# Half-row product pairs for the small corner of an fp32r split, in a mixture-of-experts stage on TensorE

## The chip, the cores and the metric

One of the cores of one Trainium2 chip runs the whole program. The metric is the device time of one execution in microseconds (us); lower is better. The profile is one more execution, with every instruction recorded.

## What is computed

The reference is an image-and-text model with two layers. Image patches are embedded and joined with looked-up text rows to 8 x 141 = 1128 tokens of width 192. Then come a two-way state-space block with a feed-forward, a quantized feed-forward, an attention of 12 heads, and a mixture of experts. The change is in the last, which computes with `flat` = 1128 x 192, hidden width 768:

```python
def _expert(xf, W1, W2, W3):
    gate = jnp.minimum(xf @ W1, LIMIT)
    up = jnp.clip(xf @ W3, -LIMIT, LIMIT)
    return jax.nn.silu(gate) * up @ W2
scores = jnp.sqrt(jax.nn.softplus(flat @ gate_w))
_, indices = jax.lax.top_k(scores + gate_bias, K)        # K = 2 of 8 experts
...
y = _expert(flat, w1s, w2s, w3s)                          # shared expert
# routed: the same with w1, w2, w3 of each token's two experts, weighted and added
```

## The kernel before

Five engines run hand-written queues, tied by semaphores. The experts' part, at the end, is a list `ITEMS` of 21 items: five "shared" ones (the shared expert on 256 tokens, the last on 128), then sixteen "routed" ones, each 256 slots of tokens that one expert has been given. `SLOTS` is 256, `KH` is 6, `P` is 128, `DA` and `DB` are 128 and 64 (the width 192 is cut at 128).

**A step.** An item has six steps (`n = g * KH + m`), each for 128 of the 768 hidden columns: a gate half (q = 0) and an up half (q = 1), each summed in its own PSUM bank (`bank[2 * (n % 2) + q]`), so that two steps can be in flight. The function `up` (L1880 on) issues the steps on TensorE.

**The split.** The products are in fp32r, a reduced form that runs in one pass. To keep accuracy, tokens and weights are split in a lead (the value rounded to fp32r) and a rest (value minus lead). Rows 0 to 127 of the width take three products: lead x lead (L1909), lead x rest of the tokens (L1910), rest of the weights x lead (L1911). The last 64 rows of the width fill only half of the 128 rows, so they are laid down twice: `x_both` holds the tokens' lead in partitions 0 to 63 and their rest in 64 to 127, and the weights' block (`2 * P` to `4 * P` of its columns) holds the same 64 rows twice. L1912 multiplies the weights' lead with `x_both`, which gives lead x lead and lead x rest at once; L1913 multiplies the weights' rest with `x_both`, which gives rest x lead and, in the other half, rest x rest, a term that L1909 to L1911 leave out. That makes five products of 128 rows, 128 output columns and 256 moving columns per half, ten per step.

**Who makes the operands.** ACT's `lead_x(g)` (L1276) copies the tokens of item g to `x_lead` (L1287) and to the lower half of `x_both` (L1288), each with a count on the semaphore `x_lead`; DVE's `rest_x` (L2715) waits for the two counts and subtracts to `x_rest` (L2725) and to the upper half of `x_both` (L2726), with counts on `x_rest`, for which `up` waits. Both are double buffered. For routed items the source is PSUM: POOL gathers token rows by indirect DMA (L844), and TensorE turns them (`turn_slots`, L1932 and L1933). ACT's `lead_w` (L1298) rounds a step's weights four steps ahead, DVE's `rest_w` (L2732) makes the rest two steps ahead; `w_lead` and `w_rest` have four buffers. The experts' weights come by indirect DMA from POOL (L823), three buffers deep, asked for when an earlier item has been finished.

**What follows a step.** ACT takes Silu of the gate half (L1328) after the fifth product, DVE clips the up half (L2655) after the tenth and multiplies both (L2666). TensorE's step n waits for Silu and clip of step n - 2 (`g_silu`, `u_clip`).

**Order on TensorE.** `up(g)`, then the turning of the next routed item's tokens, then `down(g - 1)` (L1949, two times six f32 products of 192 columns, recorded as 24; half as many for the item with 128 tokens), then `up(g + 1)`. In the shared items the router's small work is put between steps: the gate products (L1872 with 128 rows and L1873 with 64), the counting (L1903, L1904) and the placing products (L1919) in the fifth item; the router's arithmetic stands between the steps of DVE's queue. ACT's order after an item's last Silu and `lead_w` is `lead_x(g + 1)`, then `output(g - 1)` (L1315), which waits for the down projection.

**Other places that the prediction reads.** The attention's score products (L1754) have 64 rows: for each pair of heads one product reads partitions 0 to 63 and the next 64 to 127, into two banks; an f32 product is recorded as two. Before and behind them stand fp32r projections of 128 rows (L1716 to L1720, 282 columns). L1774 and L1775 are transposes of 128 and 96 rows. L1633 and L1634 are a feed-forward's f32 products, of 128 rows and, for the bias, of one row.

Of the kernel before, what the change touches and what calls it, by code (L numbers as in the profile page):

```python
# [17 lines left out]
P = 128  # L18
# [56 lines left out]
def build(nc, i, out):  # L75
    ctx = ExitStack()
    with ctx:
# [52 lines left out]
        def reduced(name, at, width, end, size):  # L130

            return nc.alloc_sbuf_tensor_at(name, [P, width], F32R, offset=end - 4 * (size - at))
# [51 lines left out]
        def lead_rest(name, base, at, width, dt):  # L184
# [158 lines left out]
        XH = [reduced(f"x_lead{k}", KH * SLOTS * 2 + k * SLOTS, SLOTS, big2_end, N2) for k in range(2)]  # L343
        XR = [reduced(f"x_rest{k}", KH * SLOTS * 2 + (2 + k) * SLOTS, SLOTS, big2_end, N2) for k in range(2)]
        XB = [reduced(f"x_both{k}", KH * SLOTS * 2 + (4 + k) * SLOTS, SLOTS, big2_end, N2) for k in range(2)]
        WAT = [(KH * SLOTS * 2 + 6 * SLOTS + k * 2 * BLK, big2_end, N2) for k in range(2)] \
            + [(1024 + k * 2 * BLK, creg_end, 5120) for k in range(2)]
        WH = [reduced(f"w_lead{k}", at, BLK, end, size) for k, (at, end, size) in enumerate(WAT)]
# [530 lines left out]
        def _(act):  # L879
# [395 lines left out]
            def lead_x(g):  # L1275

                kind, c = ITEMS[g]
                w = TOK(kind, c)
                if kind == "shared":
                    a, b = XTa[:, c * SLOTS:c * SLOTS + w], XTb[0:DB, c * SLOTS:c * SLOTS + w]  # L1280
                else:
                    act.wait_ge(S["slots_turned"], c + 1)
                    o = bank[6 + c % 2]
                    a, b = o[:, 0:SLOTS], o[0:DB, SLOTS:2 * SLOTS]
                if g >= 2:
                    act.wait_ge(S["gu_mm"], 2 * KH * (g - 1))
                nc.scalar.copy(XH[g % 2][:, 0:w], a).then_inc(S["x_lead"], 1)  # L1287
                nc.scalar.copy(XB[g % 2][0:DB, 0:w], b).then_inc(S["x_lead"], 1)  # L1288

            def lead_w(n):  # L1290

# [56 lines left out]
        def _(pe):  # L1348
# [531 lines left out]
            def up(g):  # L1880
# [1 line left out]
                kind, c = ITEMS[g]  # L1882
                w = TOK(kind, c)
                pe.wait_ge(S["x_rest"], 2 * (g + 1))
                xh, xr, xb = XH[g % 2][:, 0:w], XR[g % 2][:, 0:w], XB[g % 2][:, 0:w]
                for m in range(KH):
                    n = g * KH + m
                    if kind == "routed":
# [12 lines left out]
                    if n == KH + 5:  # L1901
                        pe.wait_ge(S["picked"], 1)
                        mm(bank[7][:, 0:RT], before[:, :], MB[:, :, :].rearrange("p t e -> p (t e)"), start=True, stop=True)  # L1903
                        mm(bank[7][:, RT:2 * RT], ones[:, :], MB[:, :, :].rearrange("p t e -> p (t e)"), start=True, stop=True)\  # L1904
                            .then_inc(S["counted"], 1)
                    for q in range(2):
                        o = bank[2 * (n % 2) + q][:, 0:w]
                        a, b = slice(q * P, (q + 1) * P), slice((2 + q) * P, (3 + q) * P)
                        mm(o, wh[:, a], xh, start=True, stop=False)  # L1909
                        mm(o, wh[:, a], xr, start=False, stop=False)  # L1910
                        mm(o, wl[:, a], xh, start=False, stop=False)  # L1911
                        mm(o, wh[:, b], xb, start=False, stop=False)  # L1912
                        mm(o, wl[:, b], xb, start=False, stop=True).then_inc(S["gu_mm"], 1)  # L1913
                    if n == PLACED:
                        pe.wait_ge(S["spread"], 3)
                        o = bank[6][:, 0:2 * CHUNKS]
# [7 lines left out]
            def turn_slots(j):  # L1924

                pe.wait_ge(ld_slots[j % 2], 16 * GCH * (j // 2 + 1))
                if j >= 2:
                    pe.wait_ge(S["x_rest"], 2 * (FIRST + j - 1))
                o = bank[6 + j % 2]
                for q in range(GCH):  # L1930
                    x = XG[:, j % 2, q * D:(q + 1) * D]
# [33 lines left out]
        def _(dve):  # L1965
# [749 lines left out]
            def rest_x(g):  # L2715
# [5 lines left out]
                else:  # L2721
                    o = bank[6 + c % 2]
                    a, b = o[:, 0:SLOTS], o[0:DB, SLOTS:2 * SLOTS]
                dve.wait_ge(S["x_lead"], 2 * (g + 1))
                v.tensor_tensor(XR[g % 2][:, 0:w], a, XH[g % 2][:, 0:w], ALU.subtract).then_inc(S["x_rest"], 1)  # L2725
                v.tensor_tensor(XB[g % 2][DB:P, 0:w], b, XB[g % 2][0:DB, 0:w], ALU.subtract).then_inc(S["x_rest"], 1)  # L2726

# [233 lines left out]
```

## Time and profile before

| | us |
|---|---|
| median of 3 runs | 735.29 |
| lowest, highest | 730.75, 736.48 |
| the profiled execution | 732.9 |
| its span, first to last instruction | 730.9 |
| mean granted clock of TensorE over the span | 0.934 of full |

Engines: PE is TensorE's products, PEld its weight loads, which overlap them, DVE is VectorE, ACT ScalarE, POOL GpSimd. Times in rows are us from the span's start, unless marked ns. A timeline row gives start, length, engine, line, operation, out<-in, shapes, count of merged instructions and, in brackets, the engine's idle time before it and what released it. Products are pipelined and their ends are modelled: their lengths overlap, and starts say more than lengths. A granted clock of 1.00 is TensorE's higher level, 2.4 GHz.

### The profile page before, as it was taken

Reading aid. Unit: us, or ns where it says so; the run is one execution under the profiler, and the core shown is the slowest. Engines: PE = TensorE matmul, PEld = TensorE weight load, DVE = VectorE, ACT = ScalarE, POOL = GpSimd, SP = SyncE. Lnnn points to the kernel's source line nnn. Section 1 sums busy time; section 2 is a strip of 40 time slices with the busy share of each in tenths; the row PEclk is TensorE's granted clock in tenths of the full one; section 3 lists DMA queues with packets and bytes.
Section 4 is the critical chain, followed back from the end, with each engine's and each line's share of the span. In section 5 each row is a group of like instructions: output and inputs, shape, how many; then the busy total and the mean of one; then the engine's idle time right before and its main releaser. Section 6 shows DMA issues by size and latency. Waiting matters only on the chain.

```text
span 730.9 us, 13424 instructions
## 1 busy us (share of the span) xinstructions
PE 633.8 (87%) x4912; PEld 566.1 (77%) x4912; DVE 490.0 (67%) x1269; ACT 383.2 (52%) x875; POOL 277.1 (38%) x292
## 2 busy tenths in 40 slices
PE   3759898899899556568999999989999999999993
PEld 3659775569898432357888888979999999999993
DVE  3668688674604877657777785488587768677761
ACT  1349876873433466455665643442255656556540
POOL 5340525344301415042323353001244756666633
PEclk9959999999999756679999999999999999999997
DMA  6600000215000580300000110103095876768733
GB/s 181 120 1 5 1 1 1 98 50 147 1 0 1 148 150 0 120 0 5 4 4 4 25 72 2 48 1 120 19 320 153 250 234 198 261 177 254 200 95 69
DMA packets 27585, 64.67 MB, mean 88 GB/s; under 512 B 5951, under 2 KB 19152, under 8 KB 25184
## 3 DMA queue, kind: packets, MB, share of 16 engines
q0 software_dynamic: 12640, 46.90, 21.8%
q1 hardware_dynamic: 13116, 16.04, 8.3%
q10 hardware_dynamic: 1764, 0.88, 0.5%
q8 instruction: 39, 0.64, 0.4%
q14 instruction: 26, 0.21, 0.1%
HBM read 58.55 MB, written 5.74 MB: 88 GB/s over the span
## 4 chain that ended last, share of the span: by engine, by line
PE 46%; DVE 6%; issue 2%; ACT 2%; POOL 1%; DMA 0%; POOLq 0%; DVEq 0%; ACTq 0%
PE bank L1949 11%; PE bank L1909 4%; PE bank L1912 4%; PE bank L1913 4%; PE bank L1910 4%; PE bank L1911 4%; PE bank L1818 2%; PE bank L1754 2%; PE bank L1797 2%; DVE amx L2559 1%; PE bank L1774 1%; PE bank L1804 1%; PE bank L1716 1%; PE bank L1780 1%; DVE big L2565 1%
## 5 line engine op out<-in xcount | busy, mean ns | idle before, releaser
L2655 DVE TENSOR_SCALAR big<-bank 128x256 f32<-128x256 f32 (+1 forms) x126 | 52.3, 415 | 52.9 <-PE bank L1913 52.6
L1328 ACT ACTIVATE big<-bank 128x256 f32<-128x256 f32 (+1 forms) x126 | 47.5, 379 | 48.9 <-PE bank L1913 48.9
L811 POOL TENSOR_TENSOR big<-big,arc 128x423 f32<-128x423 f32 (+1 forms) x48 | 37.8, 814 | 73.6 <-DVE arc L2579 73.6
L837 POOL DMA_INDIRECT total<-big,goal x32 | 54.1, 1692 | 23.9 <-issue 17.5
L1909 PE MATMUL bank<-x_lead,w_lead 128*128 128x256 f32 x192 | 56.4, 294 | 0.0
L1912 PE MATMUL bank<-x_both,w_lead 128*128 128x256 f32 x192 | 54.4, 283 | 0.0
L1913 PE MATMUL bank<-x_both,w_rest 128*128 128x256 f32 x192 | 54.1, 282 | 0.0
L1911 PE MATMUL bank<-x_lead,w_rest 128*128 128x256 f32 x192 | 54.1, 282 | 0.0
L1910 PE MATMUL bank<-x_rest,w_lead 128*128 128x256 f32 x192 | 54.0, 281 | 0.0
L2666 DVE SCALAR_TENSOR_TENSOR big<-big 128x256 f32<-128x256 f32 (+1 forms) x126 | 50.4, 412 | 0.0
L844 POOL DMA_INDIRECT big<-x_rows,origin x32 | 34.0, 1061 | 33.9 <-DVE goal L2712 20.1
L1298 ACT CAST w_lead<-wreg 128x512 fp32r<-128x512 f32 x60 | 37.2, 620 | 14.0 <-DMA wreg<-in_e_gate_up,expert 6.7
L2732 DVE TENSOR_TENSOR w_rest<-wreg,w_lead 128x512 fp32r<-128x512 f32 x60 | 41.6, 693 | 0.3
L2559 DVE TENSOR_REDUCE amx<-bank 128x3 f32<-128x423 f32 (+1 forms) x48 | 25.9, 540 | 22.9 <-PE bank L1754 15.2
L1949 PE MATMUL bank<-wreg,big 128*128 128x192 f32 x240 | 40.7, 326 | 0.0
L1949 PEld LDWEIGHTS bank<-wreg,big 128*128 128x128 f32 x240 | 38.8, 190 | 0.0
L1315 ACT ACTIVATE big<-bank,share 128x192 f32<-128x192 f32 x32 | 11.8, 418 | 50.9 <-PE bank L1949 50.9
L1909 PEld LDWEIGHTS bank<-x_lead,w_lead 128*128 128x128 f32 x192 | 36.5, 190 | 0.3 <-DVE x_both L2726 0.2
L1912 PEld LDWEIGHTS bank<-x_both,w_lead 128*128 128x128 f32 x192 | 36.5, 190 | 0.0
L1913 PEld LDWEIGHTS bank<-x_both,w_rest 128*128 128x128 f32 x192 | 36.4, 190 | 0.0
L1910 PEld LDWEIGHTS bank<-x_rest,w_lead 128*128 128x128 f32 x192 | 36.4, 189 | 0.0
L1911 PEld LDWEIGHTS bank<-x_lead,w_rest 128*128 128x128 f32 x192 | 36.3, 189 | 0.0
(542 smaller groups left out, 2022.9 us busy)
## 6 DMA issues: line engine op xcount, KB each, us to landing
big<-in_patches SPq DMA_DIRECT2D x2, 768.0 KB, 8.6
areg<-in_e_gate_up SPq DMA_DIRECT2D x1, 1536.0 KB, 6.5
shared_lead<-in_e_gate_up POOLq DMA_DIRECT2D x1, 1536.0 KB, 7.2
wreg<-in_ffn_w SPq DMA_DIRECT2D x1, 1152.0 KB
ffw_lead<-in_ffn_w POOLq DMA_DIRECT2D x1, 1152.0 KB, 7.8
out<-total SPq DMA_DIRECT2D x2, 423.0 KB
wreg<-in_in_w SPq DMA_DIRECT2D x2, 419.0 KB
wreg<-in_in_w SPq DMA_DIRECT2D x4, 209.5 KB
```

The lines of the kernel that those rows point to most:

```text
L811: pool.tensor_tensor(o, o, arc[0:r, 18 * (b % 2) + 3 * g:18 * (b % 2) + 3 * g + q].unsqueeze(2).to_broadcast([r, q, L]), ALU.mult).then_in ...
L837: pool.indirect_dma_start(out=total, in_=YS[:, j % 2, q * D:(q + 1) * D], in_offset=None, out_offset=bass.IndirectOffsetOnAxis(ap=goal[:, ...
L1328: nc.scalar.activation(GS[:, n % 3, 0:w], bank[2 * (n % 2)][:, 0:w], ACT.Silu).then_inc(S["g_silu"], 1)
L1909: mm(o, wh[:, a], xh, start=True, stop=False)
L1910: mm(o, wh[:, a], xr, start=False, stop=False)
L1911: mm(o, wl[:, a], xh, start=False, stop=False)
L1912: mm(o, wh[:, b], xb, start=False, stop=False)
L1913: mm(o, wl[:, b], xb, start=False, stop=True).then_inc(S["gu_mm"], 1)
L1949: last = mm(result(g, q), HH[:, g % 2, at:at + P], W[:, W2 + k * D:W2 + (k + 1) * D], start=k == 0, stop=k == KH - 1)
L2655: v.tensor_scalar(UM[:, n % 3, 0:w], bank[2 * (n % 2) + 1][:, 0:w], 10.0, -10.0, ALU.min, ALU.max).then_inc(S["u_clip"], 1)
L2666: v.scalar_tensor_tensor(out=HH[:, g % 2, m * SLOTS:m * SLOTS + w], in0=GS[:, n % 3, 0:w], scalar=SILU_LIMIT, in1=UM[:, n % 3, 0:w], op0=A ...
L2732: v.tensor_tensor(WL[n % 4][:, :], weights(g)[:, m * BLK:(m + 1) * BLK], WH[n % 4][:, :], ALU.subtract)\
```

## The change

Per step, the two products with `x_both` and the weights' rest (L1913, once for each half) go. In their place, ahead of the step's other products, stand two products of 64 rows: the gate's with the lower half of the weights' rest and of `x_both`, the up half's with the upper half of the weights' rest and a second copy of the tokens' lead in partitions 64 to 127 (`x_upper`, two buffers, in free room of `creg`). They open the two sums (`start=True`); the other eight products follow as before, and the gate half's last one is now the sixth of the step, the up half's the tenth. The term rest x rest of the last 64 rows is no longer in the sum. ACT's `lead_x` makes three copies in place of two, the waits on `x_lead` count by three, and TensorE's `up` and `turn_slots` wait for it as well.

```diff
+        XU = [reduced(f"x_upper{k}", 3200 + k * SLOTS, SLOTS, creg_end, 5120) for k in range(2)]
...
                 nc.scalar.copy(XH[g % 2][:, 0:w], a).then_inc(S["x_lead"], 1)
                 nc.scalar.copy(XB[g % 2][0:DB, 0:w], b).then_inc(S["x_lead"], 1)
+                nc.scalar.copy(XU[g % 2][DB:P, 0:w], b).then_inc(S["x_lead"], 1)
...
                 pe.wait_ge(S["x_rest"], 2 * (g + 1))
-                xh, xr, xb = XH[g % 2][:, 0:w], XR[g % 2][:, 0:w], XB[g % 2][:, 0:w]
+                pe.wait_ge(S["x_lead"], 3 * (g + 1))
+                xh, xr, xb, xu = XH[g % 2][:, 0:w], XR[g % 2][:, 0:w], XB[g % 2][:, 0:w], XU[g % 2][:, 0:w]
...
+                    gu = [bank[2 * (n % 2) + q][:, 0:w] for q in range(2)]
+                    mm(gu[0], wl[0:DB, 2 * P:3 * P], xb[0:DB], start=True, stop=False)
+                    mm(gu[1], wl[DB:P, 3 * P:4 * P], xu[DB:P], start=True, stop=False)
                     for q in range(2):
-                        o = bank[2 * (n % 2) + q][:, 0:w]
                         a, b = slice(q * P, (q + 1) * P), slice((2 + q) * P, (3 + q) * P)
-                        mm(o, wh[:, a], xh, start=True, stop=False)
-                        mm(o, wh[:, a], xr, start=False, stop=False)
-                        mm(o, wl[:, a], xh, start=False, stop=False)
-                        mm(o, wh[:, b], xb, start=False, stop=False)
-                        mm(o, wl[:, b], xb, start=False, stop=True).then_inc(S["gu_mm"], 1)
+                        mm(gu[q], wh[:, a], xh, start=False, stop=False)
+                        mm(gu[q], wh[:, a], xr, start=False, stop=False)
+                        mm(gu[q], wl[:, a], xh, start=False, stop=False)
+                        mm(gu[q], wh[:, b], xb, start=False, stop=True).then_inc(S["gu_mm"], 1)
...
                 if j >= 2:
                     pe.wait_ge(S["x_rest"], 2 * (FIRST + j - 1))
+                    pe.wait_ge(S["x_lead"], 3 * (FIRST + j - 1))
...
-                dve.wait_ge(S["x_lead"], 2 * (g + 1))
+                dve.wait_ge(S["x_lead"], 3 * (g + 1))
```

## Rows read from the trace of the kernel before

**Rows 1.** Page, part 1: busy us (share of the span), instructions by engine.

```profile
PE 633.8 (87%) x4912; PEld 566.1 (77%) x4912; DVE 490.0 (67%) x1269; ACT 383.2 (52%) x875; POOL 277.1 (38%) x292
```

**Rows 2.** Stretches: length, busy us and instructions by engine, granted clock, DMA share, GB/s.

```profile
542.73:703.72 160.99, 160.99 (x1233) 160.83 (x1233) 122.61 (x282) 94.70 (x222) 95.21 (x77) 1.00 0.72 213
355.00:440.00 85.00, 83.28 (x944) 72.35 (x943) 66.01 (x172) 47.33 (x137) 32.58 (x40) 1.00 0.07 23
```

**Rows 3.** Chain of waits from 566 to 600: its shares by line.

```profile
by line: PE bank L1949 33.5%; PE bank L1912 12.8%; PE bank L1909 12.6%; PE bank L1913 12.6%; PE bank L1910 12.6%; PE bank L1911 12.5%; PE bank L1932 1.9%; PE bank L1933 1.9%
```

**Rows 4.** Timeline of PE, one routed item: start, length, engine, line, out<-in.

```profile
577.16 0.41 PE L1909 MATMUL bank<-x_lead,w_lead 128*128 128x256 f32 x1
...
578.47 0.28 PE L1909 MATMUL bank<-x_lead,w_lead 128*128 128x256 f32 x1
...
579.66 0.28 PE L1909 MATMUL bank<-x_lead,w_lead 128*128 128x256 f32 x1
...
584.86 4.07 PE L1949 MATMUL bank<-big 128*128 128x192 f32 x24
588.62 0.41 PE L1909 MATMUL bank<-x_lead,w_lead 128*128 128x256 f32 x1
```

**Rows 5.** Timeline of DVE in that item; [idle before <-releaser].

```profile
579.86 0.42 DVE L2655 TENSOR_SCALAR big<-bank 128x256 f32<-128x256 f32 x1 [0.16 <-PE bank L1913]
...
581.13 0.42 DVE L2655 TENSOR_SCALAR big<-bank 128x256 f32<-128x256 f32 x1
...
586.45 0.42 DVE L2726 TENSOR_TENSOR x_both<-bank,x_both 64x256 fp32r<-64x256 f32 x1
```

**Rows 6.** Timeline of ACT in that item.

```profile
577.57 0.73 ACT L1315 ACTIVATE big<-bank,share 128x192 f32<-128x192 f32 x2 [3.27 <-PE bank L1949]
...
581.80 0.62 ACT L1298 CAST w_lead<-wreg 128x512 fp32r<-128x512 f32 x1 [0.96 <-DMA wreg<-in_e_gate_up,expert]
...
585.41 0.36 ACT L1288 CAST x_both<-bank 64x256 fp32r<-64x256 f32 x1
```

**Rows 7.** Groups by line, PE: busy us, mean ns, idle us before them.

```profile
L1909 PE MATMUL bank<-x_lead,w_lead 128*128 128x256 f32 x192 | 56.4, 294 | 0.0
...
L1909 PE MATMUL bank<-x_lead,shared_lead 128*128 128x256 f32 (+1 forms) x60 | 18.6, 310 | 3.1 <-issue 1.4 <-DVE big L2655 0.8 <-ACT big L1328 0.7
```

**Rows 8.** Timelines of PE and PEld, 128-row projection to 64-row scores.

```profile
335.51 0.29 PE L1720 MATMUL bank<-xa_both,qk_both_rest 128*128 128x282 f32 x1
335.73 0.99 PE L1754 MATMUL bank<-big 64*128 64x141 f32 x12
...
335.73 0.78 PEld L1754 LDWEIGHTS bank<-big 64*128 64x128 f32 x12 [0.16 <-issue]
```

**Rows 9.** Timeline of PE, transposes to scores and scores to projection.

```profile
375.98 0.49 PE L1774 MATMUL bank<-identw,big 128*128 128x128 f32 x3
376.30 0.25 PE L1775 MATMUL bank<-identw,big 96*128 96x96 f32 x1
376.48 0.99 PE L1754 MATMUL bank<-big 64*128 64x141 f32 x12
377.40 0.40 PE L1716 MATMUL bank<-xa_lead,qk_lead 128*128 128x282 f32 x1
377.63 0.29 PE L1717 MATMUL bank<-xa_rest,qk_lead 128*128 128x282 f32 x1
```

**Rows 10.** Timeline of PE, the gate products, 64 and 128 rows in turn.

```profile
463.27 0.39 PE L1873 MATMUL bank<-gatew,XTb 64*128 64x8 f32 x2
463.59 0.39 PE L1872 MATMUL bank<-gatew,XTa 128*128 128x8 f32 x2
```

**Rows 11.** Timeline of PE, a one-row product between 128-row ones.

```profile
221.98 0.59 PE L1634 MATMUL bank<-ffb,ones 1*128 1x192 f32 x2
222.50 0.59 PE L1633 MATMUL bank<-wreg,big 128*128 128x192 f32 x2
```

**Rows 12.** Timeline of PE, the first turn of gathered rows.

```profile
528.76 0.30 PE L1932 MATMUL bank<-identw,big 128*128 128x128 f32 x1 [1.09 <-DMA big<-x_rows,origin]
```

## The prediction

> **What bounds the kernel now.** I went from the page (which engine) to the stretches, then to the chain and the timelines of one routed item, and last to places where TensorE already changes between 128-row and 64-row products.
>
> The page has PE busy 87% of the span and no other engine over 67% [rows 1]. The change touches only `up`, so the question is what PE's time is worth there. In the routed stretch PE has no gap: 160.99 of 160.99 us at clock 1.00, with DVE at 122.61 and ACT at 94.70 [rows 2]. The chain over 566 to 600 is PE alone [rows 3]. So each of the fourteen regular routed items between 542.73 and 703.72 costs what PE's queue costs, 11.46 us (577.16 to 588.62) [rows 4].
>
> Each product is shown 0.28 long though they follow each other faster: what one costs is a start-to-start distance, not a duration. Step starts lie 1.19 us apart (578.47, 579.66) [rows 4], ten products of 0.119. DVE's cycle for a step (clip, product, rest of the weights) is 1.27 us (579.86, 581.13) [rows 5]. That is longer than PE's 1.19, and is caught up under the down projection; it is the next limit were `up` faster. ACT waits 0.96 us for the next expert's weights within an item [rows 6], the second limit.
>
> In the shared items (466.12 to 533) it is mixed: PE's first products of a half have 3.1 us of idle before them, put down to DVE, ACT and issue [rows 7]; there the router's arithmetic on DVE and the table loads on ACT stand between the steps.
>
> **What goes and comes in a step.** Before: ten full products. After: a pair (64 rows by 128 columns, moving 64x256, lower and upper half, two banks) and eight full products. The number of instructions is the same. Counted by slots the two members share one, and 0.119 us a step goes. That is right only if they run at once and if getting in and out of half-row products is free.
>
> *Do the members run at once?* L1754, the score products, has the very shape: 64*128, halves in turn, two banks. Twelve records take 0.99 us [rows 8]. One after another every 0.12 they would need 11 x 0.12 + 0.28 = 1.6. So they go two by two, about every 0.12 us. Theirs are plain f32, the new ones fp32r; if the latter don't pair, one slot of 0.12 comes back. I take the pair as one slot plus 0.01.
>
> *What does it cost to get in and out?* Full to half: the last full product, L1720 (282 columns, one pass like ours), starts at 335.51; the next weight load and product, L1754, start at 335.73, 0.22 later, and PEld was idle 0.16 before it for "issue", with no semaphore in play [rows 8]. For 256 columns that is 26 columns less to stream, 0.21. Besides, the load no longer hides under the product before it: in the other direction the first product after the crossing is 0.40 long in place of 0.29 (L1716 against L1717), 0.11 of waiting for its own weights [rows 9]. Half to full: the last L1754 starts at 376.48 + 0.99 - 0.28 = 377.19, L1716 at 377.40, again 0.21, and the 0.11 [rows 9]. So a crossing puts 0.31 to 0.32 us between two working starts where 0.119 was: +0.20 each way.
>
> Is it the rows, or only a change of source? L1775, with 96 rows, follows the 128-row L1774 at the usual distance: the two batches before it give three starts of 0.11 between 375.98 and 376.30; after it comes L1754 with 64 rows, 0.18 later [rows 9]. Bounds: the gate products, two records of 128 rows and two of 64 in turn, take 0.32 per two (463.27, 463.59) [rows 10], where two loads in line would take 0.22: +0.10 a crossing, the lower one, since 8 columns leave nothing to stream out. From above, f32 with 192 columns: the two records of L1634 (one row) last from 221.98 to 222.50, 0.52 [rows 11], against 2 x 0.157 for such records in line (24 in 3.76 us [rows 4]): +0.21. I take 0.20, from L1720, the row nearest in columns and passes.
>
> Two pages of the Trainium skill pull apart here. "TensorE: Matmul & The Clock Gate", Part 3, gives a packed group the time of one product plus about 4 ns a tile, with no term for reaching it; by that a step gains 0.12. "TensorEngine Tiling (Array Packing)", Key Properties, says that changing the tiling mode drains the array. The crossings bear out the second; the first holds inside the pair.
>
> New step: 7 x 0.119 between the eight full ones, 2 x 0.315, 0.01 for the pair: 1.47 us against 1.19, **+0.28**. It is above DVE's cycle of 1.27, so nothing hides it. In step 0 of an item the crossing comes from the down projection, with the same surcharge.
>
> **The sum.**
> - Routed, 96 steps (192 records per product line [rows 7]): 96 x 0.28 = +26.9.
> - Shared, 24 steps of 256 tokens: 24 x 0.28 = 6.7, less the 3.1 of idle [rows 7]. The crossings eat that first, since PE waits there for a chain on DVE and ACT which this very step does not feed: +3.6. Bounds: 1.8 (each of some eight waits also covers up to 0.2 beyond the idle shown) and 6.7 (none covers anything).
> - Shared, 6 steps of 128 tokens: 128 columns less to stream, a crossing is worth 0.15, a step 0.19. Five of them lie behind the placing products, and at their end PE waits 1.09 us for the gathered rows [rows 12], which POOL fetches at its own pace: hidden. The sixth costs +0.2. Were the cover gone, +0.95.
> - The third copy of `lead_x`, 21 times, 0.36 long [rows 6]. Behind it on ACT stands `output`, which began at 577.57 after 3.27 of idle [rows 6]. DVE's `rest_x` now waits for three copies; it ended at 586.45 + 0.42 = 586.87, and PE took up the item at 588.62 [rows 4, 5]: 1.75 of cover, and ACT had the second copy done at 585.77, before DVE came to it, so most of the third is hidden from DVE too. Where half a down projection covers it (the item at 542.73) it can show: +0.2 once. With no cover left it would be 21 x 0.36 = 7.6.
> - The new waits on PE ask for copies that DVE has already waited for: nothing. From above, a wait could lengthen a first product as an item's first is lengthened, 0.41 against 0.28 [rows 4], 35 x 0.13 = 4.6. No DMA is issued or moved; POOL's and SP's queues only see later semaphores. With a longer item the weights land earlier in it, so ACT's 0.96 goes, off the path.
>
> 26.9 + 3.6 + 0.2 + 0.2 = +30.9 us. The profiled execution took 732.9 us (span 730.9); it would be 763.8. The median shown is 735.3, 2.4 above it, so I forecast **766 us**, +4.2%. For this case alone, a crossing of 0.17 to 0.23 and a shared part of 2 to 7 give 757 to 775.
>
> **Rivals.**
> 1. *The pair is free to reach* (faster): a step falls to 1.07 us. For: such pairs do run at once. Against: all crossings above. In full, 120 x 0.12 = 14.4, a routed period of 10.75. But the weights for the next item, landed 4.64 us into this one (581.80 [rows 6]), come a fixed time after earlier items and would land later by what the period shrinks; the Silu behind ACT's wait, done 0.9 later still, then holds PE's step 5, due at 5.5. Solved for the period: T = (16.1 - T) + 1.0 + 5.2, about 11.15. Gain 14 x 0.31, and some 3 outside: 7 us, 728. It decides where two crossings together cost less than 0.11. The packing model named above is this rival. Chance 0.08.
> 2. *A crossing costs the gates' 0.10*: a step +0.09, 120 x 0.09 less 1.5 of waits: 745. For: rows 10. Against: rows 8 and 9, with columns nearer ours. 0.08.
> 3. *fp32r members don't pair*: 0.12 more in some 110 steps, +13: 779. For: every such pair here is f32. Against: nothing in their rows hints at the type. 0.10.
> 4. *The clock falls* with a less dense PE, whose mean over the whole span is 0.934 of full: a step at the lower level costs about twice, over +100 us if it stayed. Against: the attention stretch, full of such crossings, ran at 1.00 [rows 2]. 0.03.
>
> **How the numbers follow.** The forecast holds 0.71. 743 to 781 leaves out rivals 1 and 4 and some tail, under 2 in 10. A measurement of this kernel tells about 1% (7.4 us) from no change. Faster by more: most of rival 1, 0.07. Within 1%: its rest and the low half of rival 2, 0.05. Slower: 0.88.
>
> **What would show it.** In a routed item's timeline: the two half-row products start within 0.01 us; the pair's weight load starts 0.2 us behind the last full product, idle for "issue"; the first product after each crossing is about 0.1 longer than the rest; step starts 1.47 apart; period near 13.1; DVE idle in every step; ACT's wait for weights gone. Step starts under 1.2 and a period of 11.1 to 11.5 would make the forecast wrong at its main term; 1.59 would be rival 3.

## The result, and the profile after

| | before | after |
|---|---|---|
| median of 4 runs, us | 733.82 | 763.93 |
| lowest, highest | 730.75, 736.48 | 762.34, 765.36 |
| the profiled execution | 732.9 | 764.14 |
| its span | 730.9 | 762.1 |
| mean granted clock over the span | 0.934 | 0.928 |

The kernel after is slower: the ratio is 1.042, with a 95% interval of 1.038 to 1.046. By the profiled executions it is +31.2 us, where the forecast had +30.9. Here and in the experiments, executions that fell into a slower state of the chip are left out of every median and ratio.

In the kernel after, the pair is L1911 and L1912, and the eight full products are L1915 to L1918. The other lines move by two to six: the down projection is L1955, the turns L1938 and L1939, Silu L1331, the weights' lead L1301 and their rest L2738, the clip L2661, the three copies L1289 to L1291. First its page, part 1, as [rows 1]:

```profile
PE 669.6 (88%) x4912; PEld 568.9 (75%) x4912; DVE 497.7 (65%) x1269; ACT 398.0 (52%) x896; POOL 279.7 (37%) x292
```

PE has 36 us more of busy time with the same number of instructions, and its weight loads take hardly more (568.9 against 566.1). So nothing was added for PE to do; the same work follows itself less closely. The timeline of PE in a routed item says where, against [rows 4]:

```profile
590.46 0.28 PE L1916 MATMUL bank<-x_rest,w_lead 128*128 128x256 f32 x1
590.57 0.29 PE L1917 MATMUL bank<-x_lead,w_rest 128*128 128x256 f32 x1
590.70 0.28 PE L1918 MATMUL bank<-x_both,w_lead 128*128 128x256 f32 x1
590.91 0.38 PE L1911 MATMUL bank<-x_both,w_rest 64*128 64x256 f32 x1
590.91 0.38 PE L1912 MATMUL bank<-x_upper,w_rest 64*128 64x256 f32 x1
591.22 0.39 PE L1915 MATMUL bank<-x_lead,w_lead 128*128 128x256 f32 x1
591.44 0.29 PE L1916 MATMUL bank<-x_rest,w_lead 128*128 128x256 f32 x1
...
592.37 0.38 PE L1911 MATMUL bank<-x_both,w_rest 64*128 64x256 f32 x1
```

The two members of the pair start together (590.91). From the last full product to the pair are 0.21 us, from the pair to the next full product 0.31, and from that to its follower 0.22, where the distance between full products is 0.12. The first product after each crossing is 0.38 or 0.39 long and the others 0.28, as L1716 was against L1717 in [rows 9]. A step starts 1.46 us after the last one (590.91, 592.37). The weight loads (PEld) in the same place:

```profile
590.46 0.19 PEld L1917 LDWEIGHTS bank<-x_lead,w_rest 128*128 128x128 f32 x1
590.58 0.19 PEld L1918 LDWEIGHTS bank<-x_both,w_lead 128*128 128x128 f32 x1
590.90 0.18 PEld L1911 LDWEIGHTS bank<-x_both,w_rest 64*128 64x128 f32 x1
590.91 0.18 PEld L1912 LDWEIGHTS bank<-x_upper,w_rest 64*128 64x128 f32 x1
591.22 0.19 PEld L1915 LDWEIGHTS bank<-x_lead,w_lead 128*128 128x128 f32 x1
```

Within a run of full products the load for the next one starts 0.11 to 0.12 before that product does: L1918's load at 590.58, its product at 590.70. At a crossing the load starts with its product (590.90 and 590.91; 591.22 and 591.22). Within a run it comes 0.01 behind the start of the product before it (590.57, 590.58); at a crossing it comes 0.20 behind the last full product (590.70) and 0.31 behind the pair (590.91). So it no longer hides under the products of the other form. By groups, beside [rows 7]:

```profile
L1915 PE MATMUL bank<-x_lead,w_lead 128*128 128x256 f32 x192 | 64.0, 334 | 0.0
L1918 PE MATMUL bank<-x_both,w_lead 128*128 128x256 f32 x192 | 54.1, 282 | 0.0
...
L1911 PE MATMUL bank<-x_both,w_rest 64*128 64x256 f32 x96 | 36.6, 381 | 0.1
L1912 PE MATMUL bank<-x_upper,w_rest 64*128 64x256 f32 x96 | 36.5, 380 | 0.0
...
L1301 ACT CAST w_lead<-wreg 128x512 fp32r<-128x512 f32 x60 | 37.2, 620 | 5.9
```

L1915's mean of 334 ns is that of two kinds, about 0.39 behind the pair (the gate half) and 0.28 within the step (the up half). L1301's idle time no longer names a DMA: ACT's wait for the next expert's weights is gone from the routed items. DVE, which had been close to the limit, now idles in every step (its timeline, clips 1.47 apart):

```profile
592.47 0.42 DVE L2661 TENSOR_SCALAR big<-bank 128x256 f32<-128x256 f32 x1 [0.44 <-PE bank L1918]
...
593.94 0.42 DVE L2661 TENSOR_SCALAR big<-bank 128x256 f32<-128x256 f32 x1
```

The chain of waits from 577 to 610, by line, beside [rows 3], is still PE alone, and L1915 and L1911, the products behind a crossing, now hold 38%. (The down projection's 23.7% can't be set against its 33.5% there: this window holds two of them and that of [rows 3] three. One takes 3.9 us in an item of 13.09, 30%, and took 3.8 in one of 11.49, 33%.)

```profile
by line: PE bank L1955 23.7%; PE bank L1915 22.4%; PE bank L1911 16.0%; PE bank L1918 12.2%; PE bank L1917 12.2%; PE bank L1916 12.2%; PE bank L1939 1.3%; PE bank L1938 1.3%; PE bank L1912 0.1%
```

**Where the 31.2 us lie.** The first routed item starts at 538.82 (before: 533.00), the first shared one at 465.81 (466.12). So the shared items hold +6.1, and from 538.82 to the end it is 223.3 us against 197.9, +25.4. The stretches of the kernel after, in the columns of [rows 2]: fourteen routed items, and four stretches of the shared part.

```profile
550.49:733.79 183.30, 183.30 (x1234) 160.04 (x1232) 127.84 (x282) 106.51 (x237) 97.70 (x77) 1.00 0.67 187
...
466.00:474.00 8.00, 8.00 (x49) 6.89 (x48) 1.64 (x5) 2.36 (x5) 0.00 (x0) 0.79 0.37 108
474.00:481.00 7.00, 6.72 (x29) 5.66 (x29) 5.62 (x20) 3.24 (x7) 0.00 (x0) 0.52 0.01 2
481.00:532.00 51.00, 50.16 (x350) 44.07 (x349) 35.04 (x136) 15.47 (x39) 5.12 (x5) 1.00 0.13 47
532.00:539.00 7.00, 7.00 (x38) 6.70 (x37) 2.34 (x8) 1.78 (x5) 5.46 (x6) 0.76 0.77 225
```

The same stretches of the kernel before:

```profile
466.00:474.00 8.00, 8.00 (x51) 7.73 (x51) 1.65 (x5) 2.22 (x5) 0.00 (x0) 0.79 0.36 108
474.00:481.00 7.00, 5.57 (x44) 5.16 (x43) 6.45 (x23) 4.35 (x9) 0.00 (x0) 1.00 0.01 2
481.00:528.70 47.70, 44.46 (x341) 43.27 (x340) 35.23 (x138) 14.12 (x36) 6.07 (x6) 1.00 0.15 52
528.70:533.00 4.30, 4.24 (x29) 4.27 (x29) 0.84 (x2) 0.63 (x2) 3.13 (x4) 1.00 0.77 180
```

Fourteen routed items take 183.30 us where they took 160.99 [rows 2], at clock 1.00 both times. In the shared part two stretches stand out that were at 1.00 before: 474 to 481, now at 0.52, and 532 to 539, now at 0.76. The step starts, read from both timelines, split the shared part:

| from, to | before | after | more |
|---|---|---|---|
| start of the part to step 4 | 466.12 to 476.65 | 465.81 to 476.61 | 0.3 |
| steps 4 and 5 | to 479.32 | to 481.41 | 2.1 |
| steps 6 to 23, 256 tokens | to 516.71 | to 521.02 | 2.2 |
| steps of 128 tokens, wait for the gathered rows | to 528.76 | to 533.12 | 0.05 |
| turns and first down projection | to 533.00 | to 538.82 | 1.5 |

Steps 4 and 5 and the last row lie in the stretches of low clock. Two rows of the kernel after show it: full products follow each other every 0.21 us there.

```profile
477.50 0.41 PE L1916 MATMUL bank<-x_rest,shared_lead 128*128 128x256 f32 x1
477.71 0.41 PE L1917 MATMUL bank<-x_lead,shared_rest 128*128 128x256 f32 x1
```

### The profile page after: what moved, and what is told of

The parts are those of the page before. It is cut to its first block, busy times and chain, and to the rows that moved or that the text cites. A ratio compares the mean times of both kernels' runs of the same rounds, so it can differ in the third digit from the quotient of the medians.

```text
span 762.1 us, 13445 instructions
## 1 busy us (share of the span) xinstructions
PE 669.6 (88%) x4912; PEld 568.9 (75%) x4912; DVE 497.7 (65%) x1269; ACT 398.0 (52%) x896; POOL 279.7 (37%) x292
## 4 chain that ended last, share of the span: by engine, by line
PE 50%; DVE 5%; ACT 2%; issue 2%; POOL 1%; POOLq 0%; DVEq 0%; ACTq 0%
PE bank L1955 10%; PE bank L1915 7%; PE bank L1911 5%; PE bank L1916 4%; PE bank L1918 4%; PE bank L1917 4%; PE bank L1821 2%; PE bank L1757 2%; PE bank L1800 1%; DVE amx L2565 1%; PE bank L1777 1%; PE bank L1807 1%; PE bank L1719 1%; PE bank L1783 1%; DVE big L2571 1%
## 5 line engine op out<-in xcount | busy, mean ns | idle before, releaser
L2661 DVE TENSOR_SCALAR big<-bank 128x256 f32<-128x256 f32 (+1 forms) x126 | 52.6, 418 | 69.3 <-PE bank L1918 62.8
L1331 ACT ACTIVATE big<-bank 128x256 f32<-128x256 f32 (+1 forms) x126 | 47.5, 378 | 85.2 <-PE bank L1918 85.2
L1915 PE MATMUL bank<-x_lead,w_lead 128*128 128x256 f32 x192 | 64.0, 334 | 0.0
L839 POOL DMA_INDIRECT total<-big,goal x32 | 53.0, 1657 | 26.9 <-issue 19.0
L1918 PE MATMUL bank<-x_both,w_lead 128*128 128x256 f32 x192 | 54.1, 282 | 0.0
L846 POOL DMA_INDIRECT big<-x_rows,origin x32 | 35.8, 1120 | 38.0 <-DVE goal L2718 21.4
L1915 PEld LDWEIGHTS bank<-x_lead,w_lead 128*128 128x128 f32 x192 | 36.0, 188 | 12.3
L2738 DVE TENSOR_TENSOR w_rest<-wreg,w_lead 128x512 fp32r<-128x512 f32 x60 | 41.1, 685 | 0.3
L1955 PE MATMUL bank<-wreg,big 128*128 128x192 f32 x240 | 40.7, 326 | 0.0
L1301 ACT CAST w_lead<-wreg 128x512 fp32r<-128x512 f32 x60 | 37.2, 620 | 5.9
L1955 PEld LDWEIGHTS bank<-wreg,big 128*128 128x128 f32 x240 | 38.8, 190 | 0.0
L1911 PE MATMUL bank<-x_both,w_rest 64*128 64x256 f32 x96 | 36.6, 381 | 0.1
L1912 PE MATMUL bank<-x_upper,w_rest 64*128 64x256 f32 x96 | 36.5, 380 | 0.0
L1918 PEld LDWEIGHTS bank<-x_both,w_lead 128*128 128x128 f32 x192 | 36.2, 189 | 0.0
```

The costliest lines, as they stand in the source:

```text
L839: pool.indirect_dma_start(out=total, in_=YS[:, j % 2, q * D:(q + 1) * D], in_offset=None, out_offset=bass.IndirectOffsetOnAxis(ap=goal[:, ...
L1331: nc.scalar.activation(GS[:, n % 3, 0:w], bank[2 * (n % 2)][:, 0:w], ACT.Silu).then_inc(S["g_silu"], 1)
L1911: mm(gu[0], wl[0:DB, 2 * P:3 * P], xb[0:DB], start=True, stop=False)
L1915: mm(gu[q], wh[:, a], xh, start=False, stop=False)
L1918: mm(gu[q], wh[:, b], xb, start=False, stop=True).then_inc(S["gu_mm"], 1)
L1955: last = mm(result(g, q), HH[:, g % 2, at:at + P], W[:, W2 + k * D:W2 + (k + 1) * D], start=k == 0, stop=k == KH - 1)
```

## The experiments

The theory: a crossing between 128-row and 64-row products costs PE about 0.2 us, at any place and in both directions, and nothing else of the change costs or gains. The rivals: the loss is that of the third copy and the waits, or of the pair's place at the head of the step, or the pair doesn't overlap; and, for what the change could have brought, that ACT and DVE would have taken over as the limit at once. The runs stood on more than one chip: the kernel before has a median of 733.3 us beside the first four, 738.6 to 738.9 beside the next seven and 738.3 beside the last. Each ratio is against the runs of its own chip. Where a period is named, it is that of the regular routed items, from one turn to the next: 11.49 before, 13.09 after.

**1. The copies and waits alone.** From the kernel after; the pair goes, and the fifth full product comes back.

```diff
-                    mm(gu[0], wl[0:DB, 2 * P:3 * P], xb[0:DB], start=True, stop=False)
-                    mm(gu[1], wl[DB:P, 3 * P:4 * P], xu[DB:P], start=True, stop=False)
...
-                        mm(gu[q], wh[:, b], xb, start=False, stop=True).then_inc(S["gu_mm"], 1)
+                        mm(gu[q], wh[:, b], xb, start=False, stop=False)
+                        mm(gu[q], wl[:, b], xb, start=False, stop=True).then_inc(S["gu_mm"], 1)
```

> Only the third copy of lead_x and the waits that count by three are in; the products are those of the kernel before. Theory (crossings between 128-row and 64-row products cost, nothing else does): within 1 us of the kernel before, routed item period 11.5 us. Rival (copies and waits hold up PE at item starts): the part of the +30 us that is theirs, 1 us at least.

Measured: 732.76 us, ratio 0.998 (0.995 to 1.001), period 11.49. The item that starts on half a down projection's cover takes 9.97 between its turns in place of 9.71; that is the one place where the third copy shows. The copies and waits are not where the time went.

**2. The order alone.** The pair gives way to two full products at the same place.

```diff
-                    mm(gu[0], wl[0:DB, 2 * P:3 * P], xb[0:DB], start=True, stop=False)
-                    mm(gu[1], wl[DB:P, 3 * P:4 * P], xu[DB:P], start=True, stop=False)
+                    mm(gu[0], wl[:, 2 * P:3 * P], xb, start=True, stop=False)
+                    mm(gu[1], wl[:, 3 * P:4 * P], xb, start=True, stop=False)
```

> The changed kernel, with the two opening products of a step over all 128 rows (the full lower and upper block with x_both) in place of the pair: order, copies and waits of the change, no crossing. Theory: step starts 1.19 us apart, time that of the kernel before, 732 to 737. Rival (the new order costs, since the gate half ends one product later and the first products read the weights' rest, which is ready last): near 764.

Measured: 732.06 us, ratio 0.999 (0.996 to 1.002), period 11.49. Same order, same change of bank with every product at the head, same semaphores: only the 64 rows are missing, and with them all of the loss.

**3. Both members in the same half.** The up half's product reads the lower half as well.

```diff
-                    mm(gu[1], wl[DB:P, 3 * P:4 * P], xu[DB:P], start=True, stop=False)
+                    mm(gu[1], wl[0:DB, 3 * P:4 * P], xb[0:DB], start=True, stop=False)
```

> The changed kernel, but the up half's 64-row product reads the lower half too, so that both use the same 64 rows of TensorE. Same crossings, same sums. Theory (the pair runs at once only because the halves are opposite): one slot more a step, 1.57 to 1.58 us, in 110 to 120 steps, 776 to 778. Rival (the halves don't matter): 764.

Measured: 781.56 us, from one execution, so there is no interval. Period 13.79, 0.12 us a step above the kernel after. That is as expected; the whole is some 4 us above the 776 to 778. Up to the first turns of the routed part it is 7.0 us behind the kernel after (540.09, 533.12), of which its 30 steps make up 3.6 at most; there the lower clock lasts longer (0.50 in 474 to 481 and 0.63 in 530 to 537). Its timeline of PE:

```profile
572.72 0.28 PE L1918 MATMUL bank<-x_both,w_lead 128*128 128x256 f32 x1
572.93 0.39 PE L1911 MATMUL bank<-x_both,w_rest 64*128 64x256 f32 x1
573.15 0.28 PE L1912 MATMUL bank<-x_both,w_rest 64*128 64x256 f32 x1
573.36 0.39 PE L1915 MATMUL bank<-x_lead,w_lead 128*128 128x256 f32 x1
```

In one half they go one after the other; in opposite halves they go together. So the overlap is real in fp32r too, and worth one slot. The crossings are as before: L1918 to L1915 is 0.64 us here and 0.52 in the kernel after, and what is over is the second member's slot.

**4. 96 rows.** Both products read partitions 0 to 95, which adds half of the rest x rest term to the sum.

```diff
-                    mm(gu[0], wl[0:DB, 2 * P:3 * P], xb[0:DB], start=True, stop=False)
-                    mm(gu[1], wl[DB:P, 3 * P:4 * P], xu[DB:P], start=True, stop=False)
+                    mm(gu[0], wl[0:96, 2 * P:3 * P], xb[0:96], start=True, stop=False)
+                    mm(gu[1], wl[0:96, 3 * P:4 * P], xb[0:96], start=True, stop=False)
```

> The changed kernel with the two opening products over 96 rows (0 to 95), which adds half of the term rest x rest. Theory (96 rows run like 128, no crossing; no pairing either): time of the kernel before, 732 to 737, step 1.19. Rival (any product with fewer rows than the array makes it wait): as the changed kernel or slower, 764 to 778.

Measured: 734.17 us, ratio 1.001 (0.998 to 1.004), period 11.47. Its timeline of PE:

```profile
570.17 0.28 PE L1918 MATMUL bank<-x_both,w_lead 128*128 128x256 f32 x1
570.28 0.28 PE L1911 MATMUL bank<-x_both,w_rest 96*128 96x256 f32 x1
570.40 0.28 PE L1912 MATMUL bank<-x_both,w_rest 96*128 96x256 f32 x1
570.52 0.28 PE L1915 MATMUL bank<-x_lead,w_lead 128*128 128x256 f32 x1
```

A product of fewer than 128 rows is not what costs; 96 rows follow 128 and are followed by them every 0.12 us, as L1775 after L1774 in [rows 9].

**5. Half as many crossings.** The pair stands at the end of even steps and at the start of odd ones, so that two pairs meet.

```diff
-                    mm(gu[0], wl[0:DB, 2 * P:3 * P], xb[0:DB], start=True, stop=False)
-                    mm(gu[1], wl[DB:P, 3 * P:4 * P], xu[DB:P], start=True, stop=False)
+                    if n % 2:
+                        pair(True)
...
+                    if n % 2 == 0:
+                        for last in pair(False):
+                            last.then_inc(S["gu_mm"], 1)
```

> The changed kernel with the pair at the end of even steps and at the start of odd ones, so that two pairs stand together and there are two crossings in two steps in place of four. Same products, same sums. Theory (a crossing costs 0.20, a half-row pair one slot): two steps take 15 x 0.119 + 2 x 0.315 + 0.12 = 2.53 us in place of 2.92; 120 x 0.19 = 23 us less than the changed kernel at most, 741 to 746, still slower than the kernel before; DVE's cycle of 1.27 a step is then met just so and may give some us back. Rival (the cost is one of each half-row pair): 764.

Measured: 752.04 us, ratio 1.019 (1.017 to 1.021), period 11.93. Its timeline of PE where two pairs meet:

```profile
576.85 0.28 PE L1924 MATMUL bank<-x_both,w_lead 128*128 128x256 f32 x1
577.06 0.39 PE L1913 MATMUL bank<-x_both,w_rest 64*128 64x256 f32 x1
577.07 0.38 PE L1914 MATMUL bank<-x_upper,w_rest 64*128 64x256 f32 x1
577.29 0.28 PE L1913 MATMUL bank<-x_both,w_rest 64*128 64x256 f32 x1
577.29 0.28 PE L1914 MATMUL bank<-x_upper,w_rest 64*128 64x256 f32 x1
577.50 0.38 PE L1921 MATMUL bank<-x_lead,w_lead 128*128 128x256 f32 x1
```

From full to full it is 0.65 us for four half-row products, against 0.52 for two: the second pair costs one slot of 0.13 and no crossing. A step is 0.07 above before, as expected. The whole is slower than that makes it. Of the profiled execution's +15.3, 3.3 lie before the first routed item, 6.1 in that item and 5.9 behind it. The item itself takes 15.80 us where before took 9.73. DVE and ACT stood still up to 540, and PE waited 2.44 us for DVE in it; the clock over the item is 0.78, at its lower level from 540.9 to 547.7, which is worth about the rest:

```profile
539.91 0.56 DVE L2758 TENSOR_TENSOR H<-H,bank 128x384 f32<-128x384 f32 x1 [5.26 <-remote]
```

"Remote" is a releaser that the profile doesn't name. It is taken up again in runs 8 to 12.

**6. Twice as many crossings.** Each half ends with its own 64-row product; no two stand together.

```diff
-                        mm(gu[q], wh[:, b], xb, start=False, stop=True).then_inc(S["gu_mm"], 1)
+                        mm(gu[q], wh[:, b], xb, start=False, stop=False)
+                        half, x = (slice(DB, P), xu) if q else (slice(0, DB), xb)
+                        mm(gu[q], wl[half, b], x[half], start=False, stop=True).then_inc(S["gu_mm"], 1)
```

> The changed kernel with each 64-row product at the end of its own half: four crossings a step in place of two, no pair. Theory: a step takes 6 x 0.119 + 4 x 0.315 = 1.97 us, +0.51 against the changed kernel, 49 us in 96 routed steps and 10 to 15 in the shared ones: 820 to 830. Rival (the cost is the missing overlap in the pair, not the crossing): 764 + 0.12 x 120 = 778.

Measured: 842.34 us, ratio 1.140 (1.138 to 1.142), period 16.05, which is 0.76 a step above before: four crossings of 0.19 and no slot saved. That part came as expected; 96 x 0.76 = 73 of the 109 us of the spans lie there. The shared part took the rest, more than its 30 steps make up (23 at most):

```profile
467.00:570.01 103.01, 103.01 (x459) 83.71 (x459) 45.10 (x167) 23.08 (x54) 11.57 (x12) 0.73 0.19 63
```

It took 66.88 before. The granted clock over it is 0.73, against 0.97 over the same part before; in the routed stretch it is 1.00 here too.

**7. The pair left out.** Eight products a step; the term weights' rest x tokens' lead of the last 64 rows is missing from the sum.

```diff
-                    mm(gu[0], wl[0:DB, 2 * P:3 * P], xb[0:DB], start=True, stop=False)
-                    mm(gu[1], wl[DB:P, 3 * P:4 * P], xu[DB:P], start=True, stop=False)
```

> The changed kernel without the pair at all: the term weights' rest x tokens' lead of the last 64 rows is left out, eight products a step. It shows what a free pair could give at most. Theory (the next limits stand close: DVE's 1.27 us a step, and the weights that land a fixed time after earlier items): the period settles near 11.1 us, 8 to 12 us under the kernel before, 722 to 726. Rival (PE is the only limit): 0.24 x 96 + some = 25 us less, 709.

Measured: 731.31 us, ratio 0.990 (0.988 to 0.992), 7.3 us below before and a little less than expected. Two slots fewer would be 96 x 0.24 = 23 in the routed part alone. The period alternates between 10.6 and 11.1 in the first eight regular items and is 11.0 to 11.5 in the next four, 10.98 in the mean of the twelve, where ten slots less two make 10.06. What holds it, by its waits (engine, what for, us in total, times, longest) and its stretch 570 to 703:

```profile
ACT w_lead L1301 <- DMA wreg<-in_e_gate_up,expert: 11.5, 7, 2.1
```

```profile
570.00:703.00 133.00, 125.81 (x913) 121.90 (x912) 104.15 (x240) 78.95 (x204) 87.38 (x69) 1.00 0.77 230
```

PE now has 7 us of gaps in 133, and ACT waits for weights again. The limit that lies behind PE is close. Even a product pair that took no time at all brings this kernel about one per cent. The 7.3 us are not a clean ceiling, though: trace against trace the kernel is only 1.6 us shorter than before (spans 729.3 and 730.9). The twelve periods gain 6.1, while from the first turns to the next it takes 15.5 us where before took 11.5, and the granted clock is 0.921 in both executions. In that item ACT's Silu starts 2.4 us after the product that it waits for, and PE waits 1.99 us:

```profile
537.69 0.27 PE L1916 MATMUL bank<-x_both,w_lead 128*128 128x256 f32 x1
540.08 0.38 ACT L1331 ACTIVATE big<-bank 128x256 f32<-128x256 f32 x1 [7.11 <-PE bank L1916]
```

**8. The other way round: fewer crossings in the kernel before.** If crossings cost, the old kernel has some to give. The bias product (L1634, one row) is widened to 128 with zeros below, and the gate products (L1872, L1873) are grouped by rows.

```diff
-        ffb2 = sb("ffb2", [1, D])
+        ffb2 = sb("ffb2", [P, D])
...
-                mm(o, ones[0:1, 0:rows(t)], ffb2[:, :], start=False, stop=True).then_inc(S["f2_ready"], 1)
+                mm(o, ones[:, 0:rows(t)], ffb2[:, :], start=False, stop=True).then_inc(S["f2_ready"], 1)
...
                     mm(o, XTa[:, t * P:(t + 1) * P], gatew[:, 0, :], start=t == 0, stop=False, skip_group_check=True)
+                for t in range(3 * g, 3 * (g + 1)):
+                    o = bank[4][:, t * NE:(t + 1) * NE]
```

> The kernel before with crossings taken out elsewhere: the feed-forward's bias product has 128 rows (zeros under the bias) in place of one row, and the gate products go all of 128 rows first, then all of 64, per group of three. Theory (each crossing costs 0.20 with 192 columns of f32, 0.10 with 8): 18 x 0.20 + 12 x 0.10 = 4.8 us less at most, 729 to 731. Rival (the crossings are there but hidden, since those stages wait for others): as before.

Measured: 735.43 us against 738.60, ratio 0.997 (0.995 to 0.9995), less than the 4.8 us expected at most. Set against the trace of before, the stage with the bias went from 24.3 to 21.7 us and the gates from 3.7 to 2.9, 3.4 together. Between two bias products the step went from 2.66 us (222.50, 225.16) to 2.28 (223.73, 226.01), 0.19 for each of its two crossings; so a one-row product costs the same crossing as a 64-row one. Of the 3.4 the quantized feed-forward's stage behind gave back 1.5, and from the first turns of the routed part to the next turns it took 15.95 us in place of 11.53. There ACT and DVE stood still, as in run 5:

```profile
531.42 0.37 ACT L1287 CAST x_lead<-bank 128x256 fp32r<-128x256 f32 x1 [4.21 <-remote]
```

```profile
528.60 0.29 DVE L2657 TENSOR_SCALAR big<-bank 128x128 f32<-128x128 f32 x1 [3.20 <-remote]
```

**9 to 12. Whose is the halt?** Run 9 is run 5 again, run 11 run 8 again, run 10 has the bias edit alone and run 12 the gates alone; the diffs are those above.

> The joined kernel once more. Its routed period was 11.92 us as the theory had it, but its first routed item took 15.8 us where the kernel before takes 9.7, with ACT and DVE both idle until 540 behind a releaser that the profile does not name. If that hold belongs to the kernel it comes back in the same item; if it is chance the first item takes 10 to 11 us and the time is 742 to 747 beside a kernel before of 734.

> The kernel before with only the bias product of the feed-forward over 128 rows; the gate products as before. Theory (crossings of that stage go, 2.6 us as its stage measured before; part is given back in the stage after it, which waits for DVE): 1 to 2.6 us less than the kernel before. Rival (all given back): as before.

> The kernel with fewer crossings once more. Expected 2 to 3 us under the kernel before; if the hold of ACT and DVE behind an unnamed releaser at the first routed item (it ended 4 us later there than in the kernel before, measured from the placing products) is chance, it is gone here and the profiled run lies 4 us lower.

> The kernel before with only the gate products grouped by rows, 6 crossings in place of 18. Theory (0.10 each): the two groups of gate products before the first step take 2.9 us in place of 3.7, the whole 0.8 to 1.2 us less. If the hold at the first routed item comes with the widened bias tile, it is absent here; if it comes with any kernel in which PE reaches that item earlier, it is here too, and takes the gain back.

| run | us | before on its chip | ratio (interval) | longest waits for "remote" there, us |
|---|---|---|---|---|
| 9, joined again | 751.46 | 738.93 | 1.018 (1.012 to 1.024) | 5.3 |
| 10, bias alone | 739.09 | 738.93 | 1.000 (0.998 to 1.003) | 4.2, 3.2, 2.9 |
| 11, both again | 738.13 | 738.93 | 0.999 (0.996 to 1.001) | 4.3, 3.5, 1.1 |
| 12, gates alone | 737.45 | 738.33 | 0.998 (0.997 to 1.000) | 4.2, 3.2, 2.9 |

The halt comes back in every repeat, with the same 5.3 in runs 5 and 9 and the same 4.2, 3.2 and 2.9 in runs 8, 10 and 12 (run 11, run 8's kernel, has 4.3, 3.5 and 1.1), so it is no accident of one execution; and it comes with the gates alone, where no tile grew, so the wider bias tile isn't its cause. No wait for "remote" of that size is in the traces of before, of after, and of runs 1 to 4, 6 and 7; run 7 has the shorter halt shown above, put down to PE. Runs 5 to 11 ran on one chip, and run 6 has no halt, so the chip alone doesn't make it either. But the kernel before has only the one trace, from the result, and whether it halts on the chips where its median is 5 us higher wasn't tried. It may: run 10's trace is 6.2 us longer than that of before, 4.4 of it between the first turns and the next (15.97 us against 11.53), and yet its median is that of the kernel before on its chip. Then the halt would be none of the edits' doing. The cause stays open. Run 12's timeline of PE shows that the grouping does what it should, all products in four blocks within 3.1 us where there were 3.7:

```profile
464.70 0.73 PE L1872 MATMUL bank<-gatew,XTa 128*128 128x8 f32 x6
465.37 0.83 PE L1875 MATMUL bank<-gatew,XTb 64*128 64x8 f32 x6
466.13 0.83 PE L1872 MATMUL bank<-gatew,XTa 128*128 128x8 f32 x6
466.89 1.00 PE L1875 MATMUL bank<-gatew,XTb 64*128 64x8 f32 x6
```

No version came out that beats the kernel before by a margin its own repeat confirms: run 8's interval ends just below 1, its repeat's includes 1.

## Why the prediction was right, and where it was off

**The price of a crossing** was the main term and held. Four kernels with different numbers of crossings give it from their periods (against 11.49; a saved slot is 0.119):

| kernel | crossings a step | slots saved | more per step | price of one |
|---|---|---|---|---|
| joined (run 5) | 1 | 1 | (11.93 - 11.49) / 6 = 0.07 | 0.19 |
| after | 2 | 1 | (13.09 - 11.49) / 6 = 0.27 | 0.19 |
| same half (run 3) | 2 | 0 | (13.79 - 11.49) / 6 = 0.38 | 0.19 |
| apart (run 6) | 4 | 0 | (16.05 - 11.49) / 6 = 0.76 | 0.19 |

The forecast had 0.20 from the attention's rows [rows 8, 9], and 0.01 for the pair. The nearest row in columns and passes was the right one; the gates' 0.10 [rows 10] is what is left of a crossing when 8 columns are in flight. "TensorEngine Tiling (Array Packing)" of the Trainium skill, Key Properties, says that a change of tiling mode drains the array, and the 0.21 and 0.31 us at the crossings agree with it; run 4 adds that 96 rows cost nothing here, and runs 5 and 6 that the price goes with the changes and not with the half-row products.

**The step** is 1.46 where 1.47 was forecast. The period before is 11.49, not the 11.46 of the one item that was read [rows 4]; the two together make the routed regular items +22.3 in place of 84 x 0.28 = 23.5. The twelve steps at the ends gave +3.1, near the 3.4 forecast. The routed part came to +25.4 against 26.9.

**The shared part** came to +6.1 against 3.8 (3.6 and 0.2), and here the agreement of the totals hides a wrong step. The crossings alone cost less than forecast. From step 6 to 23 they made 2.2 where 18 x 0.28 is 5.0, and up to step 4 they made 0.3. The waits covered more than the 3.1 us put down to them in [rows 7]. (The lower bound of this term is also off by its own terms: eight waits of 0.2 leave 2.0 and not 1.8.) The five 128-token steps were hidden behind the gathered rows, as forecast (0.05). What the sum lacked is the clock: 2.1 in steps 4 and 5, of which crossings at full clock would be 2 x 0.27 = 0.5, and 1.5 in the turns and the first down projection, together 1.6 + 1.5, about 3 us. Rival 4 had a lower clock as something that would stay in the routed part and cost over 100 us; in the regular items there it stayed at 1.00. It fell in two short stretches of the shared part, where before it had not. Whether the change did that, the traces of the experiments don't settle (granted clock, from the views by stretches):

| stretch | before | after | 1 copies | 2 order | 3 same half | 4 96 rows | 5 joined | 9 joined again | 6 apart | 7 left out |
|---|---|---|---|---|---|---|---|---|---|---|
| 474 to 481 | 1.00 | 0.52 | 1.00 | 1.00 | 0.50 | 1.00 | 1.00 | 0.59 | 0.50 | 0.96 |
| 530 to 537 | 1.00 | 0.76 | 1.00 | 0.81 | 0.63 | 0.76 | 0.76 | 0.76 | 1.00 | 0.76 |

In 474 to 481 the clock is low in four of the five traces of kernels with crossings in a step; in those without it is 1.00 (before, runs 1, 2 and 4, and also 8, 10, 11 and 12) or nearly so (run 7). That speaks for a link. But runs 5 and 9 are one kernel, and one execution had the low stretch and the other not, so it also varies between executions, and the 1.6 us are not shown to be the change's:

```profile
474.00:481.00 7.00, 6.66 (x36) 5.81 (x35) 5.49 (x20) 2.43 (x5) 0.00 (x0) 0.59 0.00 0
```

(That row is run 9's. The times of run 6 lie elsewhere in its work by the second stretch.) In 530 to 537 it is low too in runs 2, 4 and 7, which have no crossing in a step, so the 1.5 us there may be this execution's and not the change's; in runs 2 and 4 too it takes 1.5 us more from the first turns to the next (13.00 and 13.02 against 11.53). The crossings of the shared items proper made 0.3 + 0.5 + 2.2 + 0.05 = 3.0 us. So the term for the shared part was mis-sized by 0.8, and that the whole came out within 0.3 us is luck: about 3 us of lower clock, for which the sum had no term, made up for it and for the 1.5 that the routed part fell short. Such a term belonged into the shared part's bounds, which reached to 6.7 and so held the result for another reason.

**The pair overlaps** (rival 3 out): shown by the equal starts and by run 3, which costs the 0.12 a step that the rival put on it.

**Copies and waits** cost nothing, shown by run 1, with 0.26 us in the one item that was named.

**Rival 1's limit** was argued from ACT's wait for weights and Silu. Run 7 took out not only the crossings but the pair's slot, and gained 7.3 us by the medians and 6.1 in twelve regular periods; its mean period of 10.98, and the weights' wait that is back, bear out that 7 us is about the most there was to win. A pair that is free to reach was not run; having a slot more in each step than run 7, it should bring no more than that.

**What failed in the experiments' expectations** were mostly the parts outside the regular routed items: the halt in runs 5 and 8 to 12, and the clock of the shared part in runs 3 and 6.

## What to carry to other kernels

Count the changes between full-row and half-row products on TensorE, not the products: one excursion is two crossings, here 0.38 us for 256 fp32r columns, and a pair in opposite halves wins one slot, here 0.12. By these two numbers, an estimate that no run tried, an excursion pays from four pairs on; this kernel's step had only one to offer. Take the price from a place in the same trace where such a change already happens, with columns and passes near to those of the new one. And check first what the second-slowest engine allows: here the whole product was worth about one per cent.

## What the runs showed of the hardware that was not expected

The granted clock in the shared part was lower in the traces with more crossings, though PE was no less busy in the profile: 0.97 before, with PE busy for 62.15 of 66.88 us, 0.91 after, and 0.73 with four crossings a step, where PE was busy in all of 103.01 us. In that last kernel it lay at its lower level for 44 us on end (468.6 to 513.0), and both of its executions have the same mean, 0.911. Smaller differences are not safe to put down to the crossings: between 474 and 481 the joined kernel, with one crossing a step, had 1.00 in one execution and 0.59 in another (runs 5 and 9). In the routed stretch of regular items it was 1.00 in every kernel in the table above, with as many crossings. What sets the two parts apart wasn't tried and stays open. And six of the twelve runs had DVE and ACT halted for 3 to 5 us around the first routed item by a releaser that the profile doesn't name, mostly with the same lengths, open as well.
